# A graph kernel's second layer: the turned one-hot compared on VectorE from loaded targets, not turned on TensorE

## The reference, cut to what matters

```
Q, K, V = x@Wq+bq, x@Wk+bk, x@Wv+bv          # per node
E = edge_attr @ We + be                       # per edge
score = K[src] * Q[dst] / sqrt(12) * E
score = exp(clip(score.sum over 12, -5, 5))   # per edge and head
wV[dst] += V[src] * score ;  Z[dst] += score
x = layernorm(x + wV / (Z + 1e-6))
```

## Time and profile before

| | us |
|---|---|
| runs | 5209.57, 5227.79, 5226.73 |
| median | 5226.73 |
| profiled execution | 5248.06 |
| its span in the trace | 5246.3 |
| first layer and node stages, about | 0 to 2600 |
| second layer, about | 2600 to 5246 |

### The profile page before, as it was taken

How to read it: one execution, slowest core, us unless ns; L and a number is a source line. 1 busy time by engine, 2 the same in 40 slices (tenths; PEclk the granted TensorE clock), 3 DMA queues, 4 the chain that set the end, 5 groups by cost and what they waited for, 6 DMA issues and landing times.

```text
span 5246.3 us, 52541 instructions
## 1 busy us (share of the span) xinstructions
PE 3084.1 (59%) x16572; PEld 2872.6 (55%) x16572; DVE 1883.1 (36%) x5136; ACT 845.8 (16%) x1933; POOL 3240.7 (62%) x3330
## 2 busy tenths in 40 slices
PE   2445454554454445444566666776667676777776
PEld 2445444444444444444566666665666566666666
DVE  3223222222222222222334444444444444444444
ACT  1212222222222222222201111101101110111111
POOL 6666666666666666666466656666666566666664
PEclk9855555555555555555556666566665656665666
DMA  3111111111111111111133333333333333333333
GB/s 93 37 38 37 42 38 37 36 42 37 37 37 43 37 37 37 43 37 37 46 99 106 103 102 105 104 104 101 106 103 105 99 106 104 103 102 103 106 105 82
DMA packets 277580, 376.85 MB, mean 72 GB/s; under 512 B 140757, under 2 KB 183414, under 8 KB 277302
## 3 DMA queue, kind: packets, MB, share of 16 engines
q0 software_dynamic: 132864, 245.03, 18.2%
q1 hardware_dynamic: 144438, 128.41, 8.5%
HBM read 353.82 MB, written 19.32 MB: 71 GB/s over the span
## 4 chain that ended last, share of the span: by engine, by line
another core or an unknown queue 48%; PE 23%; issue 12%; DVE 9%; ACT 7%; DVEq 0%; ACTq 0%
PE banks L493 6%; PE banks L534 6%; PE banks L523 4%; PE banks L554 3%; ACT ex L633 3%; PE banks L543 3%; ACT relu L626 2%; DVE mt L767 2%; DVE ex L838 1%; DVE prod L902 1%; PE banks L467 1%; DVE score L917 1%; DVE onehot L742 1%; DVE prod L888 1%
## 5 line engine op out<-in xcount | busy, mean ns | idle before, releaser
L405 POOL DMA_INDIRECT rows<-key_value,src_i x1661 | 1625.2, 978 | 1051.8 <-DVE vals L894 517.2
L405 POOL DMA_INDIRECT rows<-in_x,src_i x1661 | 1614.1, 972 | 922.2 <-issue 510.1
L493 PE MATMUL banks<-onehot,ex 128*96 128x64 f32 x6644 | 1074.2, 355 | 1273.6 <-ACT ex L633 713.2
L493 PEld LDWEIGHTS banks<-onehot,ex 128*96 128x96 f32 x6644 | 1039.9, 267 | 1313.6 <-issue 1111.7
L534 PE MATMUL banks<-qw,onehot_t 128*128 128x192 f32 x1664 | 590.5, 503 | 478.4 <-ACT onehot_t L659 378.1
L534 PEld LDWEIGHTS banks<-qw,onehot_t 128*128 128x128 f32 x1664 | 435.1, 299 | 505.2 <-ACT onehot_t L659 399.3
L523 PE MATMUL banks<-we_sb,ea 97*128 97x96 f32 x3322 | 665.5, 366 | 0.3 <-issue 0.3
L523 PEld LDWEIGHTS banks<-we_sb,ea 97*128 97x128 f32 x3322 | 615.6, 276 | 0.0
L848 DVE TENSOR_TENSOR sums<-sums,banks 96x128 f32 x416 | 117.3, 282 | 1343.4 <-remote 1157.7
L554 PEld LDWEIGHTS banks<-onehot,vals 128*104 128x104 f32 x3322 | 575.7, 266 | 1.2 <-DVE vals L894 1.1
L554 PE MATMUL banks<-onehot,vals 128*104 128x64 f32 x3322 | 566.8, 343 | 1.0 <-DVE vals L894 1.0
(11 more groups left out here) (90 smaller groups left out, 1237.9 us busy)
## 6 DMA issues: line engine op xcount, KB each, us to landing
ea<-in_edge_t SPq DMA_DIRECT2D x415, 192.0 KB
rows<-in_x,src_i POOLq DMA_INDIRECT x1661
rows<-key_value,src_i POOLq DMA_INDIRECT x1661
qw<-query SPq DMA_DIRECT2D x832, 24.0 KB
key_value<-qkv SPq DMA_DIRECT2D x24, 384.0 KB
xt<-in_x_t SPq DMA_DIRECT2D x7, 672.0 KB, 11.8
query<-qkv SPq DMA_DIRECT2D x24, 192.0 KB
out<-outs SPq DMA_DIRECT2D x24, 192.0 KB
```

The source lines that it names most:

```text
L405: pool.indirect_dma_start(out=to[0:n, r, u, :], out_offset=None, in_=table, in_offset=bass.IndirectOffsetOnAxis(ap=src_i[0:n, g * G + u:g ...
L493: last = nc.tensor.matmul(ps_sum0[b][:, j, :], ex[:, b, u, j * D:(j + 1) * D], onehot[:, r, u, :], start=u == 0, stop=u == n - 1)
```

## The change

`onehot_t` is no longer turned from `onehot`. SP loads, for each half of the partitions and each group, the 128 targets of two tiles, copied to all 64 partitions of that half (`dst_row`, a ring of 4, two DMAs a group). DVE compares them with the node that belongs to the partition: `own_node[p, g] = base[g] + (p mod 64)`. The result is written straight to `onehot_t`. `turn_onehot`, its PSUM bank and semaphore, and `copy_onehot` leave. `own_node` takes the storage of `ahead`, and the limit on the ring of sums gets tighter by 512.

```diff
+                def load_targets(g):
+                    r = g % RE
+                    if g >= RE:
+                        sp.wait_ge(s_oht, g - RE + 1)
+                    for half in range(2):
+                        sp.dma_start(dst_row[half * WIN:(half + 1) * WIN, r, :, :],
+                                     tile_ids[g, half, :, P:2 * P].unsqueeze(0).to_broadcast([WIN, 2, P])
+                                     ).then_inc(s_dr[r], 16)
+                tile_ids = ids.rearrange("(g j h) c -> g h j c", j=2, h=2)
...
+                for g in range(QA):
+                    load_targets(g)
...
                         load_queries(ahead_of, nodes[ahead_of % 4])
+                        if g >= 0:
+                            load_targets(ahead_of)
...
-                def turn_onehot(g):
-                    pe.wait_ge(s_oh1, g + 1)
-                    if g:
-                        pe.wait_ge(s_oht, g)
-                    for j in range(2):
-                        last = nc.tensor.transpose(
...
                 def sum_values(g):
                     b, n = g % 2, tiles_of_group(g)
+                    pe.wait_ge(s_oh1, g + 1)
                     pe.wait_ge(s_vals, g + 1)
...
-                    if g + 2 < NG:
-                        turn_onehot(g + 2)
...
-                def copy_onehot(g):
-                    act.wait_ge(s_tr1, g + 1)
-                    if g >= 2:
-                        act.wait_ge(s_qe, g - 1)
-                    nc.scalar.copy(onehot_t[:, g % 2, :, :].rearrange("p a b -> p (a b)"), ps_t).then_inc(s_oht, 1)
...
-            V.tensor_scalar(lim[:, 2:3], lim[:, 2:3], float(RN - WIN), None, ALU.is_gt)
+            V.tensor_scalar(lim[:, 2:3], lim[:, 2:3], float(RN - WIN - CN), None, ALU.is_gt)
...
+            own_node = ahead
+            link(V.tensor_scalar(own_node[:, :], base[:, :], lane[:, 0:1], None, ALU.add))
...
+                def turned_onehot(g):
+                    r = g % RE
+                    dve.wait_ge(s_dr[r], 32 * (g // RE + 1))
+                    if g >= 2:
+                        dve.wait_ge(s_qe, g - 1)
+                    V.tensor_scalar(onehot_t[:, g % 2, :, :], dst_row[:, r, :, :], own_node[:, g:g + 1], None,
+                                    ALU.is_equal).then_inc(s_oht, 1)
...
                     if g + 2 < NG:
+                        turned_onehot(g + 2)
                         make_onehot(g + 2, s_oh1)
```

More of the change, by code:

```diff
@@ L93, in build @@
         onehot_t = sb("onehot_t", [P, 2, 2, P])
+        dst_row = sb("dst_row", [P, RE, 2, P], I32)
+        lane_i = sb("lane_i", [P, 1], I32)
+        lane = sb("lane", [P, 1])
         ea = sb("ea", [D + 1, RE, G, P])
@@ L140, in build @@
         ps_q = [banks[:, 2 + b, 0:G * D] for b in range(2)]
-        ps_t = banks[:, 4, 0:2 * P]
         ps_sum1 = [banks[0:W1, 5 + b, 0:WIN] for b in range(2)]
@@ L189, in build @@
         s_oh1 = sem("s_oh1")
-        s_tr1 = sem("s_tr1")
+        s_dr = [sem(f"s_dr{r}") for r in range(RE)]
         s_oht = sem("s_oht")
@@ L394, in _ @@
             pool.iota(iota_i[:, :], pattern=[[1, WIN]], base=0, channel_multiplier=0).then_inc(s_const, 1)
+            pool.iota(lane_i[:, :], pattern=[[0, 1]], base=0, channel_multiplier=1).then_inc(s_const, 1)
             pool.memset(ident[:, :], 1.0).then_inc(s_const, 1)
-            pool.wait_ge(s_const, 2)
+            pool.wait_ge(s_const, 3)
             pool.affine_select(out=ident[:, :], in_=ident[:, :], compare_op=ALU.is_equal, fill=0.0,
@@ L427, in _ @@
         def _(pe):
-            pe.wait_ge(s_const, 4)
+            pe.wait_ge(s_const, 5)
             pe.wait_ge(s_both, 2)
@@ L536, in query_rows @@
                     last.then_inc(s_qe, 1)
-                def turn_onehot(g):
-                    pe.wait_ge(s_oh1, g + 1)
-                    if g:
-                        pe.wait_ge(s_oht, g)
-                    for j in range(2):
-                        last = nc.tensor.transpose(
-                            ps_t[:, j * P:(j + 1) * P],
-                            onehot[:, g % RO, 2 * j:2 * j + 2, :].rearrange("p a b -> p (a b)"), ident[:, :])
-                    last.then_inc(s_tr1, 1)
                 def sum_values(g):
                     b, n = g % 2, tiles_of_group(g)
+                    pe.wait_ge(s_oh1, g + 1)
                     pe.wait_ge(s_vals, g + 1)
@@ L556, in sum_values @@
                     last.then_inc(s_sum1, 1)
-                turn_onehot(0)
                 edge_products(0)
                 query_rows(0)
-                turn_onehot(1)
                 for g in range(NG + 1):
@@ L666, in exp_scores @@
                     nc.scalar.activation(vals[:, b, 0:n, D:W1], score[:, b, 0:n, :], ACT.Exp).then_inc(s_exp1, 1)
-                copy_onehot(0)
-                copy_onehot(1)
                 for g in range(NG):
-                    if g + 2 < NG:
-                        copy_onehot(g + 2)
                     exp_scores(g)
@@ L718, in _ @@
             V.memset(sums1[:, :], 0.0).then_inc(s_zero1, 1)
-            dve.wait_ge(s_const, 4)
+            dve.wait_ge(s_const, 5)
             V.tensor_copy(iota_w[:, :], iota_i[:, :])
+            link(V.tensor_scalar(lane_i[:, :], lane_i[:, :], WIN - 1, None, ALU.bitwise_and))
+            link(V.tensor_copy(lane[:, :], lane_i[:, :]))
             dve.wait_ge(s_dst, 32)
@@ L942, in _ @@
                 dve.wait_ge(s_sum, NG)
-                make_onehot(0, s_oh1)
-                make_onehot(1, s_oh1)
+                for g in range(2):
+                    turned_onehot(g)
+                for g in range(2):
+                    make_onehot(g, s_oh1)
                 for g in range(NG + 2):
```

## The result

The changed kernel takes 5239.04 us (median of 18, 5220.34 to 5251.91), the kernel before 5223.21 us (median of 18, 5204.74 to 5235.61). The ratio is 1.0026, 95% interval 1.0014 to 1.0038: no gain, but a loss of about a quarter of a per cent. The forecast was 5145 us, 1.6% faster. The time lies in the range given; of the rivals, "nothing moves" comes nearest. The profiled execution has a span of 5245.4 us.

A forecast was written before the change was run, and what follows sets the result against it. It took the second layer as bound by a loop with POOL the steadiest clock; -100 us for the faster chain and +17 for longer gathers on 5248.06 gave 5165, less 21 to the median, rounded 5145 us; range 4960 to 5280.

The forecast's parts named there:

- nothing moves: Rival: late stretches of PE's announcements set the second layer's rate, POOL stops as before; 5200 to 5253 us, chance 0.22.
- gathers, POOL's own time between them and its pauses fill the layer: Second layer: gathers 1621.4 us, POOL's own issue 477.9 and ring waits 517.2 make 2616 of 2646 us.
- PE's pace: Second layer, between late announcements: without transposes, edge products start every 4.40 us a group instead of 4.83.
- no wait of DVE for the targets: Second layer: targets come at least 7 us before DVE wants them, so nothing was counted.
- ACT's copy worth nothing that shows: PE's 378.1 us of waiting for the copy was counted as hidden by DVE; its removal brings nothing more.
- The number of pauses: POOL's second-layer waits for a free place in the ring: about 130 instead of 145.
- what 1.4 us sooner in the open stretch buys: DVE's late second-layer iteration starts 1.4 us sooner per open stretch; worth 52 to 203 us, 100 taken.
- pauses keep their length: Lower case: POOL's pauses stay 3.57 us, late stretches keep their distance; 15 fewer pauses save 52 us.
- The loads, counted at nothing: SP's two added target loads a group find room on its queue and cost 0 us.
- The comparison, counted at 17 us: DVE's added operation, 0.35 us a group, lengthens POOL's gathers by 17 us; bounds 0 and 154 us.
- The pauses dissolve: Rival: chain outpaces POOL; half of POOL's pauses going gives 4968 us, all 4710; chance 0.18.
- DVE against POOL: Rival: comparison delays one gather a group, price 154 us; 5280 or 5380 us, mean gather over 1040 ns; chance 0.18.

The follow-up runs named there:

- e1: Changed kernel with onehot_t made for the first two groups only, no target loads or comparison after; 5273.26 us, 0.9981 of the kernel before, first kind of chip.
- e4: Changed kernel with targets loaded for the first four groups only, comparison kept; 5273.65 us, 0.9982 of the kernel before, first kind of chip.
- e9c: Changed kernel without three of four edge products and their DVE multiplication in the second layer; 5219.04 us, 1.0003 of the kernel before, first kind of chip.
- e2c: Kernel before with the two target loads a group added, unread; 5223.85 us, 1.0015 of the kernel before, first kind of chip.
- e7: Changed kernel with PE's transposes of the one-hot put back, result unread; 5347.56 us, 1.0122 of the kernel before, first kind of chip.
- e8c: Kernel before with POOL waiting after every third second-layer group until its gathers landed; 5270.62 us, 1.0116 of the kernel before, first kind of chip.
- a2: Changed kernel, unaltered, measured again on the second kind of chip; 4388.22 us, 1.0109 of the kernel before.
- e1b: Changed kernel with onehot_t made for two groups only, no later target loads or comparison, second kind of chip; 4330.7 us, 0.9971 of the kernel before.
- e5: Changed kernel with POOL gathering only the first six groups of the second layer; 4264.93 and 4345.09 us, kernel before 5285.07, first kind of chip.

## Why the prediction was wrong

**Right.** That gathers, POOL's own time between them and its pauses fill the layer; PE's pace, 4.34 and 4.42 us for 4.40; the comparison, 355 ns for 350; no wait of DVE for the targets; ACT's copy worth nothing that shows.

**Right by luck.** The number of pauses, 125 for 130, and the mean gather, 984 ns for 980 to 990. With the removal alone, from which the 130 were reckoned, there are 136 pauses and the mean gather is 951 ns (e1); with the comparison added, 127 and 984 (e4). The prediction had nothing in it that would shorten the gathers, and too little that lengthens them.

**Wrong: what 1.4 us sooner in the open stretch buys.** The prediction took "pauses keep their length" for a lower bound of 52 us and chose 100. The runs gave 12 us, with none within the interval (e1), and none against the kernel before, some 0.2% against the changed one, for a chain that is 1.7 us a group faster than before (e9c). The pauses did get fewer, and each got longer. The second layer in the profiles of the first kind, in us; the pace is the median from one group's edge products to the next where nothing is announced late, and the wait is DVE's for "remote", at the key products and the sums together:

| run | PE's pace | DVE's wait | gathers | pauses | gathers + pauses | held stretches |
|---|---|---|---|---|---|---|
| before | 4.84 | 918 | 1625 | 517 | 2142 | 140 |
| e2c, loads added | 4.83 | 981 | 1637 | 510 | 2147 | 141 |
| e7, transposes back | 4.68 | 933 | 1581 | 641 | 2222 | 105 |
| after | 4.41 | 1087 | 1634 | 509 | 2143 | 133 |
| e1, removal alone | 4.41 | 1155 | 1580 | 581 | 2161 | 136 |
| e4, no loads | 4.41 | 1006 | 1635 | 508 | 2143 | 128 |
| e9c, lighter chain | 3.13 | 1232 | 1592 | 547 | 2139 | 127 |

The faster PE's pace, the longer DVE waits for announcements: what is gained in the open stretch is waited away. The sum of gathers and pauses is the layer's time less POOL's own, so that it stays says no more than that the time does; what is worth reading is that 55 us moved from pauses to gathers (e1 to e4) without a change in time. e7, whose chain waits for a one-hot, shows that the sum isn't fixed. The prediction treated the length of a pause and the distance of the held stretches as given apart from each other, and they aren't: the pauses went from 3.57 to 4.07 us, and neither bound of its 52 to 203 us could hold.

How the two are tied is in part a reading. In the profile before, 135 of 140 held stretches end within a pause of POOL, and 135 of its 145 pauses contain such an end; half of the stretches end 2.1 to 2.4 us after its last gather; in the profile after 124 of 133 do. That fits a hold that goes on until POOL stops, which it does when the ring is full: a chain that is faster ahead of the hold would leave POOL more room (3.32 groups a pause for 2.86), and the hold would end so much later. That POOL's stop is what ends it wasn't shown; stops of 2.24 us at other times often didn't (e8c). The prediction's own remark that the first layer's far lighter chain still leaves pauses was the evidence for "nothing moves", and got 0.22.

**Costs.** The loads, counted at nothing, cost 32 us on the second kind of chip; on the first they add 0.15%, with nothing and 0.34% both within the interval. The comparison, counted at 17 us, costs 38 us on the second kind and none that shows on the first (e4 against e1). The bounds (0 and 154 us) held. The gathers that start beside the comparison lose 14 us in a2 and 19 us in the changed kernel on the first kind, near the 17; the prediction missed that the new work also shifts which gathers meet `weigh_values` and `make_onehot`. In e7, with the same loads and comparison, the gathers take 952 ns, hardly more than undisturbed. On the first kind the gathers' length was hidden by the pauses, as the gain was. Removal (-0.19%, e1) and loads (+0.15%, e2c) sum to about 0 on the first kind; the measured +0.26% is within those intervals, and what makes the difference isn't settled.

The rule that the prediction draws on from the Trainium skill, "SBUF — State Buffer", section "SBUF: two separate sides", has a condition that it leaves out: the shared pair is a lock that a VectorE operation takes in a two-port mode, or with two SBUF inputs, but then only against a GpSimd operation that reads SBUF, and whichever starts first keeps it for its whole length. That GpSimd can't write descriptors is said there of the two-port modes. The gathers read their indices (`src_i`) from SBUF, and the trace agrees for two inputs: in the profile before, a gather that starts just after `weigh_values` takes 1313 ns (96 of them, 50 to 100 ns after it), and one that starts up to 50 ns ahead of it 945 (12). For the one-source comparison, gathers that start beside it take 1007 ns in a2 (224 gathers), but 1287 ns in the changed kernel on the first kind (55), where many of them meet the one-hot right behind it as well. So it holds gathers too; in which mode it ran no run shows.

**Rivals.** "Nothing moves" has the time right, and the pauses' total (509 us for 517); their number and length did move. "The pauses dissolve" failed: a lighter chain than any the change could give (e9c) leaves 547 us of them. "DVE against POOL" is, on the second kind of chip, what happens, at 57 us for the 154 forecast (a2 against e1b), with a mean gather of 988 ns, though not by one gather a group falling into step with the comparison; the threshold of 1040 ns was reckoned from a gain of 100 us that wasn't there.

**Open.** What holds PE's announcements while POOL gathers, and why only some chips do so. The runs show that it goes with the gathers (e5) and when it ends, no more. No version that computes the whole layer beat the kernel before.

## What to carry to other kernels

When a wait ends on something that the engines' own work doesn't explain, find out what ends it before pricing a faster chain: if it ends only about when another engine's ring has filled, what is gained ahead of it can be given back. Check by leaving work out, first of the chain (e9c) and then of the engine that seems to bound it (e1 against e4): if neither changes the time, both are hidden, and a shorter pace or a shorter gather has no price there. A mean duration is no property of an operation alone: look at what the longer ones start beside. And measure an edit on more than one chip, if there is more than one: the same edit was +0.26% on one and +1.09% on another.

## What was not expected of the hardware

- The same kernel takes 5218 to 5285 us on some chips and 4339 to 4343 us on others. On the latter DVE has no waits on "remote" in the second layer of the traces taken, and POOL as good as no pauses (1.2 us at most). It isn't PE's clock: there the kernel before took 4339 to 4346 us at granted clocks from 0.62 to 0.86 over the whole run (the runs beside a2).
- Held announcements go with POOL's gathers: 122 waits of DVE's key products on "remote" in the changed kernel, 1 without the gathers.
- PE's granted clock in the second layer fell from 0.62 to 0.52 when its transposes left (0.51 in e1), and came back to 0.63 with them (e7). On the time it had no effect that shows.
- Small loads on SP's queue, 256 packets of 512 B a group, cost 32 us where POOL is the bound, though a gather that meets no DVE operation takes 945 ns with them and without: they shift which gathers meet `weigh_values` and `make_onehot`.
